# Three bf16 pieces of a matrix for the residuals of a block solve, and other places for TensorE's filler work

## Chip, cores and metric

One core of one Trainium2 chip (trn2). The metric is the device time of one execution in microseconds, as the median of the runs shown.

## What is computed

The reference is two layers of a transformer block on a (4, 256, 256) input. Layer 0 is rotary attention with 16 heads plus a mixture of experts. Layer 1 is a gated delta rule with 16 key heads of two value heads each, plus a feed-forward block with a layer norm. The change lies in layer 1's delta rule:

```python
def step(state, inp):
    q_t, k_t, v_t, b_t, d_t = inp
    state = state * d_t[..., None, None]
    Sk = jnp.einsum('bhi,bhij->bhj', k_t, state)
    delta = (v_t - Sk) * b_t[..., None]
    state = state + jnp.einsum('bhi,bhj->bhij', k_t, delta)
    o = jnp.einsum('bhi,bhij->bhj', q_t, state)
    return (state, o)
```

The kernel does not step through time. For each value head and each chunk of 128 time steps it writes all `delta` at once as the solution W of a unit triangular system, W = V + N W, where N holds the decayed products of keys (the matrix of the system with its sign turned has -1 on its diagonal).

## The kernel before

**Tiling.** Layer 1 runs one `body` for each of the 16 key heads. A head has two value heads (v = 0, 1), four batch entries (b) and two chunks of time (c). `N[v]` is a tile of 128 partitions by 4 x 3 x 128 fp32 columns: for each b the blocks chunk 0 on itself, chunk 1 on chunk 0, chunk 1 on itself. The five engines run their own programs in order and meet at semaphores; the order is written out by hand in one `body` for each engine.

**A head on TensorE** (`body`, L915). The values are turned (L776), the products of keys and queries are made (`products`, L779) while VectorE forms N (`matrices`, L1349) and GpSimd multiplies the decays by the products (`decayed`, L1628). Then `invert` (L793) builds the inverse of the triangular blocks in bf16 in six levels by doubling. In each level TensorE multiplies (L802, L812, L816), VectorE masks (L1380) and ScalarE copies back (L1161, L1165).

**The solve.** The bf16 inverse (`TT`) is only approximate, so each chunk c is solved with two corrections. Stage k = 3c + a, a = 0, 1, 2, goes:
- `apply` (L843): four bf16 matmuls for each v add the inverse times the bf16 right-hand side `Rb[v]` to a PSUM bank, where W builds up over a = 0, 1, 2.
- The bank is copied to `Wv` in fp32: for a = 0 by ScalarE (`first_w`, L1169), for a = 1, 2 by ScalarE for v 0 (`next_w`, L1174) and by VectorE for v 1 (`update`, L1399).
- `residual` (L858), a = 0, 1: four fp32 matmuls for each v of N with `Wv`. An fp32 matmul is two records in the trace.
- `left_over` (L1390) on VectorE: V plus the residual's bank, written in bf16 to `Rb[v]`.
- After a = 2 of chunk 0, `link` (L870, L1441) carries chunk 0 into chunk 1's right-hand side, which ScalarE rounds (`round_r2`, L1179). After chunk 1, `outputs` (L878) multiplies the decayed products with W, and VectorE gates (`gate_o`, L1417).

**Fillers.** So that TensorE has work while the other engines copy, it does parts of the next head between these: projections (`project`, L717; each part two records of 512 columns), the projection of z (`project_z`, L736; halves) and sums of squares (`norms`, L756). The lists `ahead`, `between`, `behind` and `closing` in `body` say which filler stands ahead of the first apply, between the two applies, behind them and behind the residuals of stage k.

**VectorE in the solve.** The convolution of the next head has three taps for each of four channel groups (`conv`, L1327; one instruction L1334 each, with two inputs in SBUF). The third group's taps and the fourth's lie in the last level of the inversion and in the stages k = 0, 1, 2 (`mid` and `end` in VectorE's `body`). `guard` (L1337) turns the sums of squares into reciprocals in stage 3.

**ScalarE in the solve.** It copies out the fourth group's projection (`conv_in(ni, 3)`), squares, and makes the next head's decays (`batch_decays`, L1197). The decays wait for `mask_done` of both v.

**GpSimd** (`body`, L1636), in this order: `decayed` for four b, `scale_y` of the last head's output (L1623), the right-hand side times the norms of the keys (L1647, L1649), the diagonal of N for both v (L1655, `affine_select`, two instructions each), and the masks of the next head's decays (`mask`, L1614; four instructions L1620). In the first head the layer norm's scale, shift and addition follow (`f_tail`, L1663).

## Time and profile before

| what | us |
|---|---|
| median of 3 runs (lowest to highest) | 1804.15 (1802.18 to 1804.24) |
| the profiled execution, its own time | 1804.3 |
| its span in the profile | 1802.3 |
| busy TensorE matmul, VectorE, ScalarE, GpSimd | 1703.3, 1316.0, 1167.9, 652.5 |
| one head of layer 1 (a period of the trace) | 70.4 |

The span runs from the first to the last instruction of the program; the execution's time holds some 2 us beside it. PE is TensorE's matmuls, PEld its weight loads, DVE is VectorE, ACT ScalarE, POOL GpSimd. A matmul's record ends about 0.17 us after its engine can take the next one, so starts tell how long the queue is held.

### The profile page before, as it was taken

The page shows a single profiled execution, that of the slowest core. Times are in us where ns is not written, and L with a number is a line of the kernel's source. Part 1 is how long each engine was busy: PE and PEld are TensorE (multiplying, and loading weights), DVE is VectorE, ACT ScalarE, POOL GpSimd, SP SyncE. Part 2 cuts the span into 40 slices and gives each one's busy share as a digit, 9 for nine tenths or more (in the row PEclk, how much of TensorE's full clock was granted, in tenths as well). Part 3 has the DMA queues.
Part 4 walks back from the last instruction along what each step waited for, and adds up shares of the span by engine and source line. Part 5 has one row for each costly group of instructions (what it writes and reads, how often), then busy time and mean ns, then how long its engine had stood idle before and what let it go on. Part 6 is the DMA issues. An engine that isn't in the chain of part 4 may idle for free.

```text
span 1802.3 us, 34261 instructions
## 1 busy us (share of the span) xinstructions
PE 1703.3 (95%) x13208; PEld 1322.5 (73%) x13208; DVE 1316.0 (73%) x2293; ACT 1167.9 (65%) x2185; POOL 652.5 (36%) x474
## 2 busy tenths in 40 slices
PE   7899999999998987999999999999999999999986
PEld 5676766767665666787787787877877877878875
DVE  7788888888866267767768767777677687677753
ACT  3335353443535465778878878887787788788762
POOL 2222213222214063615516426336246165163340
PEclk9999999999999997999999999999999999999998
DMA  3111010101103200110110101101101201111000
GB/s 138 35 55 47 33 67 33 67 33 55 46 1 105 76 19 1 37 59 25 37 56 28 36 25 60 36 25 37 59 25 36 60 25 36 38 47 36 7 2 24
DMA packets 51447, 75.16 MB, mean 42 GB/s; under 512 B 3392, under 2 KB 41792, under 8 KB 51312
## 3 DMA queue, kind: packets, MB, share of 16 engines
q1 hardware_dynamic: 51312, 73.28, 12.6%
q8 instruction: 94, 1.54, 0.3%
q14 instruction: 41, 0.34, 0.1%
HBM read 72.03 MB, written 1.25 MB: 41 GB/s over the span
## 4 chain that ended last, share of the span: by engine, by line
PE 54%; ACT 7%; DVE 6%; issue 3%; DVEq 0%
PE bank L731 12%; PE bank L911 7%; PE bank L751 5%; PE bank L866 4%; PE bank L789 3%; PE bank L802 2%; PE bank L816 2%; PE bank L812 2%; DVE d_sil L1334 2%; ACT d_dec L1133 2%; PE bank L874 2%; PE bank L887 2%; PE bank L854 2%; PE bank L888 2%; PE bank L889 2%
## 5 line engine op out<-in xcount | busy, mean ns | idle before, releaser
L1634 POOL TENSOR_TENSOR d_dec<-d_dec,d_qk 128x384 f32<-128x384 f32 x128 | 138.8, 1111 | 638.4 <-DVE d_N L1359 571.3
L1334 DVE SCALAR_TENSOR_TENSOR d_sil<-d_pre,d_w,d_sil 128x1024 f32<-128x1024 f32 x192 | 295.2, 1538 | 10.1 <-ACT d_pre L1099 9.9
L731 PE MATMUL bank<-xnT,d_w 128*128 128x512 f32 x480 | 242.4, 617 | 0.0
L189 PE MATMUL bank<-xnT,a_w 128*128 128x512 f32 x512 | 236.6, 596 | 0.0
L1380 DVE CAST_PREDICATED d_X<-tables_sb,bank 128x512 bf16<-128x512 int32 x192 | 134.3, 700 | 89.9 <-PE bank L802 76.4
L1396 DVE TENSOR_TENSOR d_Rb<-d_V,bank 128x512 bf16<-128x512 f32 x128 | 86.5, 685 | 109.8 <-PE bank L866 109.8
L489 POOL TENSOR_TENSOR a_hidc<-a_hid,a_comb 128x512 f32<-128x512 f32 x32 | 44.4, 1387 | 295.0 <-DVE a_hid L336 295.0
L189 PEld LDWEIGHTS bank<-xnT,a_w 128*128 128x128 f32 x512 | 90.6, 192 | 78.5 <-issue 78.5
L1161 ACT ACTIVATE d_T<-bank 128x512 bf16<-128x512 f32 x160 | 100.5, 628 | 65.2 <-PE bank L812 62.6
L866 PE MATMUL bank<-d_W,d_N 128*128 128x128 f32 x1024 | 130.6, 281 | 2.0 <-DVE d_W L1401 1.9
L508 ACT ACTIVATE a_sg<-a_sm 128x384 f32<-128x384 f32 x64 | 33.0, 515 | 152.0 <-DVE a_sm L341 152.0
L751 PE MATMUL bank<-d_w,xnT 128*128 128x256 f32 x512 | 130.1, 388 | 0.0
L911 PE MATMUL bank<-d_wo,d_yT 128*128 128x256 f32 x512 | 127.2, 393 | 0.9 <-ACT d_yT L1194 0.9
L866 PEld LDWEIGHTS bank<-d_W,d_N 128*128 128x128 f32 x1024 | 123.0, 193 | 3.8 <-DVE d_W L1401 2.1
L1165 ACT ACTIVATE d_TT<-bank 128x512 bf16<-128x512 f32 x192 | 119.6, 623 | 2.9 <-PE bank L816 2.9
L481 POOL TENSOR_TENSOR a_qT<-a_rot_a,a_rot_b 128x512 f32<-128x512 f32 x64 | 81.3, 1270 | 100.2 <-DVE a_rot_b L325 100.2
L731 PEld LDWEIGHTS bank<-xnT,d_w 128*128 128x128 f32 x480 | 80.0, 192 | 43.6 <-issue 43.6
L1620 POOL TENSOR_TENSOR d_dec<-d_dec,tables_sb 128x512 f32<-128x512 f32 x64 | 96.8, 1543 | 16.2 <-DMA d_dec<-decay_scratch 16.2
L911 PEld LDWEIGHTS bank<-d_wo,d_yT 128*128 128x128 f32 x512 | 93.7, 193 | 11.8 <-issue 1.2
L1098 ACT ACTIVATE d_sil<-bank,d_w 128x512 f32<-128x512 f32 x128 | 90.1, 704 | 12.8 <-PE bank L983 11.9
L325 DVE SCALAR_TENSOR_TENSOR a_rot_b<-bank,a_w,tables_sb 64x512 f32<-64x512 f32 x128 | 95.9, 750 | 1.9
L751 PEld LDWEIGHTS bank<-d_w,xnT 128*128 128x128 f32 x512 | 90.7, 192 | 8.6
(210 smaller groups left out, 4274.8 us busy)
## 6 DMA issues: line engine op xcount, KB each, us to landing
d_dec<-decay_scratch SPq DMA_DIRECT2D x32, 512.0 KB, 5.7
a_w<-w SPq DMA_DIRECT2D x16, 897.0 KB, 4.6
d_w<-w SPq DMA_DIRECT2D x16, 776.0 KB, 4.6
a_comb<-comb_scratch SPq DMA_DIRECT2D x16, 512.0 KB, 5.6
d_dec<-decay_scratch SPq DMA_DIRECT2D x32, 256.0 KB, 6.1
d_wo<-w SPq DMA_DIRECT2D x16, 256.0 KB, 3.1
f_w<-w SPq DMA_DIRECT2D x8, 256.0 KB, 4.2
x_sb<-x SPq DMA_DIRECT2D x2, 512.0 KB, 4.4
```

Of the source, the lines that this page charges most:

```text
L189: last = pe.matmul(psum[bank][:, :], wq(slot, part, k), xnT[:, k, half * HALF:(half + 1) * HALF], start=(k == 0), stop=(k == KT - 1))
L325: last = dve.scalar_tensor_tensor(two(rot_b[lo:lo + 64, n % 2, :]), two(psum[n][src:src + 64, :]), bias[src:src + 64, :], SN[src:src + 64, ...
L731: last = pe.matmul(psum[bank][:, :], cols(slot, (c * KT + k) * P, P), xnT[:, k, h * HALF:(h + 1) * HALF], start=(k == 0), stop=(k == KT - 1))
L751: last = pe.matmul(psum[n][:, q * 2 * P:(q + 1) * 2 * P], xnT[:, k, t * P:(t + 1) * P], cols(slot, OZ + k * 2 * P, 2 * P), start=(k == 0), ...
L866: last = pe.matmul(psum[5 + 2 * v][:, b * P:(b + 1) * P], N[v][:, b, 2 * c, :], Wv[v][:, b, c, :], start=True, stop=True)
L911: last = pe.matmul(psum[OUT_BANK[n]][:, q * D:(q + 1) * D], yT[v][:, t * P:(t + 1) * P], wo[slot][:, v, :], start=(v == 0), stop=(v == 1))
L1161: act.activation(left(Tm[v][:, :, :], lv).rearrange("p n g w -> p (n g) w"), psum[5 + 2 * v][:, :].rearrange("p (a w) -> p a w", w=lv), AC ...
L1165: act.activation(right(TT[v][:, :, :], lv).rearrange("p n g w -> p (n g) w"), psum[4 + 2 * v][:, :].rearrange("p (a w) -> p a w", w=lv), A ...
L1334: dve.scalar_tensor_tensor(sil[c][:, :, :], pre[c % 2][:, :, tap:tap + S], cols(slot, OC + 4 * c + tap, 1), sil[c][:, :, :], ALU.mult, ALU ...
L1380: dve.copy_predicated(left(Xp[lv][:, v], lv), mask.unsqueeze(1).broadcast_to([P, 8, 64]).rearrange("p n (g w) -> p n g w", w=lv), psum[4 + ...
L1620: last = pool.tensor_tensor(g, g, tabs["future"].unsqueeze(1).broadcast_to([P, B, P]), ALU.add)
L1634: pool.tensor_tensor(g, g, qk[b][:, :, :], ALU.mult).then_inc(s["p_done"], 1)
```

## The change

Three parts.

1. **Residuals in bf16.** The diagonal blocks of N are split into three bf16 pieces: `Nh` (ScalarE casts N, `high`), `Nm` (GpSimd subtracts Nh from N in place and casts the rest, `middle`), `Nl` (GpSimd subtracts Nm from the rest, `lowest`; it takes over the tile `Nb`, so it waits for the last level's corner). Each `apply` now gives a fresh product and not a running sum. The first product is rounded to bf16 (`W0b`), the second is rounded too (`dWb`, `change`), the third stays in PSUM. The first residual is Nh W0b + Nm W0b, the second adds Nl W0b + Nh dWb + Nm dWb in the same bank: 8 and 12 bf16 matmuls of 128 columns for each v in place of 4 fp32 ones. GpSimd adds W0b and dWb (`partial`), and VectorE adds the third product from PSUM (`total`), which `link` and `outputs` wait for.
2. **Fillers.** The list `behind` is replaced by `inner`, between the two residuals. Projections of the fourth group, z halves and norms move by one or two places, so that a stage has one filler between the applies and one between the residuals.
3. **Order on the other engines.** GpSimd's masks are parted: those of v 0 ahead of `middle`, those of v 1 behind `lowest`, ahead of the partial sums. On ScalarE the decays take other places between the copies.

```diff
+        Nh = [m.sb(f"d_Nh{v}", [P, B, 2, P], BF16) for v in range(2)]
+        Nm = [m.sb(f"d_Nm{v}", [P, B, 2, P], BF16) for v in range(2)]
+        Nl = Nb
+        W0b = [m.sb(f"d_W0b{v}", [P, B, P], BF16) for v in range(2)]
+        dWb = [m.sb(f"d_dWb{v}", [P, B, P], BF16) for v in range(2)]
...
                 for b in range(B):
                     last = pe.matmul(psum[4 + 2 * v][:, b * P:(b + 1) * P], TT[v][:, 2 * b + c, :], Rb[v][:, b, :],
-                                     start=(a == 0 and b == 0), stop=(a == 2), skip_group_check=True)
+                                     start=True, stop=True)
...
             def residual(i, v, c, a):
 
                 if a == 0:
                     pe.wait_ge(s["w0_done"], i * 4 + 2 * c + v + 1)
-                    pe.wait_ge(s["diag_done"], i * 2 + v + 1)
+                    pe.wait_ge(s["nm_done"], i * 2 + v + 1)
+                    parts = ((Nh, W0b), (Nm, W0b))
                 else:
-                    pe.wait_ge(s[f"wup_done{v}"], i * 4 + 2 * c + a)
-                for b in range(B):
-                    last = pe.matmul(psum[5 + 2 * v][:, b * P:(b + 1) * P], N[v][:, b, 2 * c, :], Wv[v][:, b, c, :],
-                                     start=True, stop=True)
+                    pe.wait_ge(s["nl_done"], i * 2 + v + 1)
+                    pe.wait_ge(s[f"dw_done{v}"], i * 2 + c + 1)
+                    parts = ((Nl, W0b), (Nh, dWb), (Nm, dWb))
+                for n, (coef, vec) in enumerate(parts):
+                    for b in range(B):
+                        last = pe.matmul(psum[5 + 2 * v][:, b * P:(b + 1) * P], coef[v][:, b, c, :], vec[v][:, b, :],
+                                         start=(a == 0 and n == 0 and b == 0), stop=(a == 1 and n == 2), skip_group_check=True)
...
-                    for c, h, li, half in ((2, 0, 2, 1), (2, 1, 3, 0), (3, 0, 5, 1)):
-                        fill[li][half].append(p(c, h))
+                    for h, (li, half) in enumerate(((2, 1), (3, 0))):
+                        fill[li][half].append(p(2, h))
+                    fill[5][1].append(part(3, 0, 0))
                     z = lambda n, half: (lambda: project_z(nxt[1], nxt[2], n, (half,)))
-                    ahead[0], between[0], behind[0] = [part(3, 1, 0)], [part(3, 1, 1)], [z(0, 0)]
-                    between[1], behind[1] = [z(0, 1)], [q(0, 0)]
-                    between[2], behind[2], closing[2] = [q(0, 1)], [q(1, 0)], [q(1, 1)]
-                    between[3] = [z(1, 0)]
+                    ahead[0], between[0], inner[0] = [part(3, 0, 1)], [part(3, 1, 0)], [part(3, 1, 1)]
+                    between[1], inner[1] = [z(0, 0)], [z(0, 1)]
+                    between[2], inner[2], closing[2] = [z(1, 0)], [q(0, 0)], [q(0, 1)]
+                    between[3], inner[3] = [q(1, 0)], [q(1, 1)]
                     between[4] = [z(1, 1)]
...
                         apply(i, 1, c, a)
-                        for f in behind[k]:
-                            f()
                         for v in range(2):
                             if a < 2:
                                 residual(i, v, c, a)
                             elif c == 0:
                                 link(i, v)
+                            if v == 0:
+                                for f in inner[k]:
+                                    f()
...
+            def high(i, v):
+                act.wait_ge(s["diag_done"], i * 2 + v + 1)
+                act.activation(Nh[v][:, :, :, :], N[v][:, :, 0:3:2, :], ACT.Copy).then_inc(s["nh_done"], 1)
...
+                for v in range(2):
+                    fill[4][v].append(lambda v=v: high(i, v))
...
-                next_w(i, 0, 1)
+                change(i, 0)
                 if nxt:
                     square(ni, 1)
                     batch_decays(ni, ns, 0)
-                    batch_decays(ni, ns, 1)
-                next_w(i, 0, 2)
-                if nxt:
-                    batch_decays(ni, ns, 2)
...
+            def total(i, v, c):
+                dve.wait_ge(s["apply_ready"], i * 12 + 6 * c + 4 + v + 1)
+                dve.wait_ge(s["wsum_done"], i * 4 + 2 * c + v + 1)
+                dve.tensor_tensor(Wv[v][:, :, c, :], Wv[v][:, :, c, :], psum[4 + 2 * v][:, :].rearrange("p (b d) -> p b d", b=B),
+                                  ALU.add).then_inc(s[f"wup_done{v}"], 1)
...
-                        if a:
-                            update(i, c, a)
+                        if a == 1:
+                            change(i, c)
+                        elif a == 2:
+                            for v in range(2):
+                                total(i, v, c)
...
+            def middle(i, v):
+
+                pool.wait_ge(s["nh_done"], i * 2 + v + 1)
+                rest = N[v][:, :, 0:3:2, :]
+                pool.tensor_tensor(rest, rest, Nh[v][:, :, :, :], ALU.subtract).then_inc(s["mid_done"], 1)
+                pool.wait_ge(s["mid_done"], i * 2 + v + 1)
+                pool.tensor_copy(Nm[v][:, :, :, :], rest).then_inc(s["nm_done"], 1)
+
+            def lowest(i, v):
+
+                pool.wait_ge(s["nm_done"], i * 2 + v + 1)
+                pool.wait_ge(s["x_ready"], i * 12 + 2 * len(LEVELS) - 2 + v + 1)
+                pool.tensor_tensor(Nl[v][:, :, :, :], N[v][:, :, 0:3:2, :], Nm[v][:, :, :, :],
+                                   ALU.subtract).then_inc(s["nl_done"], 1)
+
+            def partial(i, v, c):
+
+                pool.wait_ge(s["w0_done"], i * 4 + 2 * c + v + 1)
+                pool.wait_ge(s[f"dw_done{v}"], i * 2 + c + 1)
+                pool.tensor_tensor(Wv[v][:, :, c, :], W0b[v][:, :, :], dWb[v][:, :, :], ALU.add).then_inc(s["wsum_done"], 1)
...
                 if nxt:
-                    mask(*nxt)
+                    mask(*nxt, 0)
+                for v in range(2):
+                    middle(i, v)
+                for v in range(2):
+                    lowest(i, v)
+                if nxt:
+                    mask(*nxt, 1)
+                for c in range(2):
+                    for v in range(2):
+                        partial(i, v, c)
                 if isinstance(i, int) and i == 0:
                     f_tail()
```

## Rows read from the trace of the kernel before

**Rows 1.** The page's first line.
```profile
span 1802.3 us, 34261 instructions
```

**Rows 2.** Windows: busy us of each engine over one head, granted clock, DMA share, GB/s.
```profile
1049.20:1119.64 70.44, 68.56 (x663) 55.84 (x659) 51.90 (x77) 57.54 (x103) 31.14 (x22) 1.00 0.12 39
```

**Rows 3.** Timeline of TensorE in one head's solve: start, length, records.
```profile
1125.07 1.95 PE L866 MATMUL bank<-d_W,d_N 128*128 128x128 f32 x16
...
1126.90 0.40 PE L854 MATMUL bank<-d_Rb,d_TT 128*128 128x128 bf16 x4
...
1134.17 2.05 PE L874 MATMUL bank<-d_W,d_N 128*128 128x128 f32 x16 [0.38 <-ACT d_W L1176]
...
1136.90 0.39 PE L854 MATMUL bank<-d_Rb,d_TT 128*128 128x128 bf16 x4
...
1140.16 0.40 PE L854 MATMUL bank<-d_Rb,d_TT 128*128 128x128 bf16 x4
1140.39 1.08 PE L751 MATMUL bank<-d_w,xnT 128*128 128x256 f32 x4
1141.31 0.39 PE L854 MATMUL bank<-d_Rb,d_TT 128*128 128x128 bf16 x4
...
1144.66 0.44 PE L887 MATMUL bank<-d_W,d_dec 128*128 128x128 f32 x2
```

**Rows 4.** Timeline of ScalarE in level 4 of the inversion, idle time in brackets.
```profile
1117.51 0.60 ACT L1161 ACTIVATE d_T<-bank 128x512 bf16<-128x512 f32 x1 [1.66 <-PE bank L812]
```

**Rows 5.** Timelines of GpSimd and VectorE in the same head, single instructions and groups.
```profile
1098.64 1.04 POOL L1647 TENSOR_TENSOR d_Rb<-d_V,d_knorm 128x512 bf16<-128x512 f32 x1
...
1111.04 0.63 POOL L1655 TENSOR_SCALAR_AFFINE_SELECT d_N<-d_N 128x512 f32<-128x512 f32 x1
...
1111.64 2.23 POOL L1620 TENSOR_TENSOR d_dec<-d_dec,tables_sb 128x512 f32<-128x512 f32 x1
...
1111.64 5.93 POOL L1620 TENSOR_TENSOR d_dec<-d_dec,tables_sb 128x512 f32<-128x512 f32 x4
...
1111.11 1.63 DVE L1334 SCALAR_TENSOR_TENSOR d_sil<-d_pre,d_w,d_sil 128x1024 f32<-128x1024 f32 x1
...
1118.59 1.28 DVE L1334 SCALAR_TENSOR_TENSOR d_sil<-d_pre,d_w,d_sil 128x1024 f32<-128x1024 f32 x1
```

**Rows 6.** One line's instructions over the whole trace: ns min/median/max, first and last start.
```profile
L1620 POOL TENSOR_TENSOR d_dec<-d_dec,tables_sb x64: 1260/1272/2251, 576.1 to 1679.8; 128x512 f32<-128x512 f32 x64
...
L1682 POOL COPY d_X<-d_identb x12: 1036/1040/1041, 548.1 to 558.9; 128x1024 bf16<-128x1024 bf16 x12
...
L1626 POOL TENSOR_TENSOR x_sb<-x_sb,d_yrs x32: 1886/1896/1899, 742.7 to 1782.9; 128x1024 f32<-128x1024 f32 x32
...
L1396 DVE TENSOR_TENSOR d_Rb<-d_V,bank x128: 673/686/690, 689.6 to 1770.6; 128x512 bf16<-128x512 f32 x128
...
L1151 ACT ACTIVATE d_Nb<-d_N x32: 1048/1051/1059, 655.0 to 1728.2; 128x1024 bf16<-128x1024 f32 x32
```

**Rows 7.** Timelines of GpSimd and VectorE in the first head.
```profile
695.05 4.51 POOL L1667 TENSOR_TENSOR x_sb<-x_sb,f_gamma 128x2048 f32<-128x2048 f32 x1 [19.36 <-DVE x_sb L1460]
...
705.11 5.39 POOL L1671 TENSOR_TENSOR acc_sb<-acc_sb,x_sb 128x2048 f32<-128x2048 f32 x1
...
695.49 5.15 DVE L1334 SCALAR_TENSOR_TENSOR d_sil<-d_pre,d_w,d_sil 128x1024 f32<-128x1024 f32 x1
...
723.64 0.69 DVE L1423 TENSOR_TENSOR x_sb<-d_gated,bank 128x512 f32<-128x512 f32 x1 [0.70 <-PE bank L889]
```

**Rows 8.** Windows of the first and last head; the third-last number is the granted clock.
```profile
663.20:678.20 15.00, 8.87 (x160) 6.26 (x160) 14.90 (x28) 10.49 (x21) 12.49 (x8) 1.00 0.00 1
678.30:685.00 6.70, 5.36 (x36) 3.04 (x37) 3.32 (x6) 4.85 (x6) 0.00 (x0) 0.50 0.01 2
1754.00:1773.00 19.00, 15.20 (x141) 13.42 (x139) 9.75 (x15) 6.41 (x11) 0.00 (x0) 1.00 0.00 1
```

More of the change, by code:

```diff
@@ L907, in project_out @@
                     pe.wait_ge(s["pre_done"], nxt[2] * 8 + 4 + n - 1)
-                for q in range(2):
+                for q in parts:
                     t = 2 * n + q
@@ L933, in body @@
                         fill[li][half].append(lambda n=n: project_out(*before, n, nxt))
-                ahead, between, behind, closing = ([[] for _ in range(6)] for _ in range(4))
+                ahead, between, inner, closing = ([[] for _ in range(6)] for _ in range(4))
                 if nxt:
@@ L1494, in body @@
                     mid[2] = [cv(3, 2)]
-                    end[3] = [lambda: guard(ns, ni)]
+                    end[3].append(lambda: guard(ns, ni))
                 if first:
@@ L1613, in _, with mask @@
         def _(pool):
-            def mask(j, slot, i):
+            def mask(j, slot, i, v):
                 pool.wait_ge(dec_in[slot], j * 64 + 64)
-                for v in range(2):
-                    for c in (0, 2):
-                        g = dec[slot][v][:, :, c, :]
-                        last = pool.tensor_tensor(g, g, tabs["future"].unsqueeze(1).broadcast_to([P, B, P]), ALU.add)
-                    last.then_inc(s["mask_done"], 1)
+                for c in (0, 2):
+                    g = dec[slot][v][:, :, c, :]
+                    last = pool.tensor_tensor(g, g, tabs["future"].unsqueeze(1).broadcast_to([P, B, P]), ALU.add)
+                last.then_inc(s["mask_done"], 1)
             def scale_y(i, v):
@@ L1634, in decayed, with diagonal @@
                     pool.tensor_tensor(g, g, qk[b][:, :, :], ALU.mult).then_inc(s["p_done"], 1)
+            def diagonal(i, v):
+                pool.wait_ge(s["nb_done"], i * 2 + v + 1)
+                pool.wait_ge(s["tt1_done"], i * 2 + v + 1)
+                for c in (0, 2):
+                    n = N[v][:, :, c, :]
+                    last = pool.affine_select(n, n, pattern=[[0, B], [-1, P]], base=0, channel_multiplier=1,
+                                              compare_op=ALU.not_equal, fill=-1.0)
+                last.then_inc(s["diag_done"], 1)
+            def middle(i, v):
[13 more added lines that the diff above has]
+                pool.tensor_tensor(Wv[v][:, :, c, :], W0b[v][:, :, :], dWb[v][:, :, :], ALU.add).then_inc(s["wsum_done"], 1)
             def body(j, slot, i):
@@ L1682, in _ @@
                     pool.tensor_copy(Xp[lv][:, v, :, :], identb[:, :].unsqueeze(1).broadcast_to([P, 8, P])).then_inc(ev["ident_done"], 1)
-            mask(0, 0, 0)
+            for v in range(2):
+                mask(0, 0, 0, v)
             loop(pool, body)
```

43 lines of the change are left out of this document (19 added, 24 removed).

## The prediction, made before the changed kernel was run

> **What bounds the kernel now.** First the page: one core, a span of 1802.3 us [rows 1]. Then a window over one head of layer 1: 70.44 us, of which TensorE is busy 68.56, VectorE 51.90, ScalarE 57.54 and GpSimd 31.14 [rows 2]. So TensorE bounds a head, and GpSimd looks idle for more than half of it. That share is an average. The timeline of GpSimd shows that its work lies in one piece and that its last masks begin at 1111.64 and run for 5.93 us [rows 5]; behind them it sleeps until the next head. The solve is later: the first pair of residuals starts at 1125.07, the link of the two halves at 1134.17, the first apply of the second half at 1136.90 and the outputs at 1144.66 [rows 3]. I use this head's clock from here on.
>
> **What TensorE saves.** A pair of fp32 residuals (sixteen records) holds the queue from 1125.07 to 1126.90, 1.83 us [rows 3]. Four bf16 matmuls of the same 128 columns hold it for 0.23 (the apply from 1140.16, the filler behind it at 1140.39) [rows 3], 0.056 each. The new pairs have 16 and 24 of these: 0.90 and 1.34 us. A head has two pairs of each kind: 7.32 before, 4.48 after, 2.8 us less work. It is a gain only where nothing else is late. The fillers keep their number and are moved by a place or two; one lasts 0.92 (1140.39 to 1141.31) [rows 3].
>
> **Small terms.** ScalarE gets two castings of 1024 columns a head, 1.05 each [rows 6], behind the diagonal, in level 4 of the inversion. There it idles, 1.66 us before the copy at 1117.51 alone [rows 4]: nothing, as long as these gaps stand; without them each would delay the inversion by 1.05. It loses two copies. VectorE loses two copies and gains four totals of the kind that the residual subtraction has, 0.69 each [rows 6]. The last two lie on the path between the last apply and the outputs.
>
> **What GpSimd gains, and its price.** Behind the diagonal now stand, in this order: two masks, casting work for both v (subtract, copy, subtract, copy), two subtractions for the lowest piece, the other two masks, and four partial sums, of which two belong to the first half of the solve. A subtraction of 1024 columns with two full inputs is not in the trace. The mask adds 512 columns in 1.27 [rows 6]; right behind a release it needs 1.13 (below), so 0.14 is spent ahead of the data and 1024 columns cost 2.4. Bounds: 1.04, what a copy of 1024 bf16 columns takes, and 2.4; with one broadcast input 1024 columns took 1.90 [rows 6]. I take 2.4, since both inputs are full tiles. The copy to bf16 costs 1.04 by the nearest row, 1.90 at most. A partial sum costs 1.27, between 1.04 (the scaled 512 columns written in bf16 [rows 5]) and 1.5.
>
> **The term that decides: the taps of the convolution.** Look at 1111.04. GpSimd's diagonal takes 0.63, to 1111.67. The tap that VectorE starts at 1111.11 ends only at 1112.74, 1.07 after it; in the clear, at 1118.59, it takes 1.28 [rows 5]. The mask that GpSimd starts at 1111.64 ends at 1113.87, 1.13 after the tap [rows 5]. So the two never overlap: one holds the other off for its whole length, and with both waiting they alternate. The same shows in the first head: beside a GpSimd instruction of 4.51 a tap takes 5.15 [rows 7]. In the kernel before, a head's last six taps, from 1118.59 on, run while GpSimd sleeps. After the change the first five of them run against it. Each adds 1.07 + 0.04 - 0.14, some 1.0, to GpSimd's row, and waits itself for up to 2.4.
>
> **GpSimd's row, added up.** The first two masks end at 1113.87 and, 1.23 later, at 1115.1. Behind them: four subtractions 9.6, two copies 2.1, two masks 2.5, two partial sums 2.5, together 16.8, less 0.04 of overlap ten times, plus five taps (the third channel group's three and the fourth's first two) at 1.0: 21.3 us. The second partial sum of the first half ends at **1136.4**, the first at 1134.2. Without taps it would be 1131.5. The middle pieces are ready at 1118.5 and 1122.9, ahead of the residuals at 1125; the lowest ones at 1125.2 and 1128.6, ahead of theirs at 1129 and 1131; the last masks at 1133, which holds back ScalarE's decays (2.9 with their table load, an estimate from ScalarE's place in the queue) but not yet the rounding of the second half. So what is late is the totals. The fourth group's second tap ends at 1135.3, the first total at 1136.0, and the link of v 0 starts there instead of at 1134.17. Then come a filler, the link of v 1 (its total is ready at 1137.1) and a filler: 2 x 0.92 of links and 2 x 0.92 of fillers, and the first apply of the second half starts at 1139.7 instead of 1136.90: **+2.8 us a head**. The 1.4 us saved by two residual pairs and the filler that is already behind are in this number: TensorE has waited them away.
>
> **The second half.** From that apply to the next stage: two applies 0.45, two fillers 1.84, two short residuals 0.90, so 3.2 against 3.26. The next stage has one filler: apply and filler to 1.15, the change of v 1 is in PSUM 0.42 after its start and copied 0.69 later, at 2.3; its residual (0.67 and 0.2 until it is read) ends at 3.2, the subtraction at 3.9, the total of v 0 starts 0.1 before that and ends at 4.5. Before, 4.50. No change: the latency of the total eats the residual's gain.
>
> **First and last head.** In the first, the layer norm's three instructions on GpSimd (from 695.05 to 710.50 [rows 7]) now stand behind the partial sums, so behind the second half. The taps that they held up for some 10 us run free, TensorE is at the outputs some 10 us sooner, near 712; but the gating needs their end: 15.4 us behind 711.5 is 727, against 723.64 [rows 7], and then its four instructions run without gaps. Net +1, between -3 and +5. The last head has no taps, masks or fillers: shorter residuals against waits for partial sums, 0, between -2 and +1.
>
> **Sum.** 14 heads at +2.8 are +39, first head +1: 1804.3 (the profiled execution, 2.0 above its span; the median of runs is 1804.15) gives 1844.
>
> **A page's price.** The Trainium skill (GPSIMD Engine Reference, section 3.1) gives some 2.6 cycles at 1.2 GHz per element for two inputs, a floor that comes from its one read port, and names no type. By it the subtraction would take 2.2 us (an estimate from that page), 0.2 under the value taken, and the sum would be 1838; it speaks against the first rival below. No row here has a bf16 input in such an instruction.
>
> **Rivals.** (1) *GpSimd reads bf16 cheaper*: at 1.90 the four subtractions are 2.0 sooner, and the taps fall elsewhere: +0.8 to +2.1 a head, 1816 to 1834, about 1826. For it: the broadcast row. Against: full tiles stand at 2.4. (2) *GpSimd is in time* (the other side): place, the totals of the first half, which VectorE could reach at 1132.0 and 1132.6 if no tap waited. It decides if the second partial sum ends by 1132.6, that is if a subtraction costs 1.1 or less. Then the saved residuals count in the first half alone, -0.45 a head, and -1 in the last: 1797. At 1.3 it is no change. For it: a copy of the same size takes 1.04. Against: every instruction with two inputs. (3) *The clock falls as well*: TensorE would idle 1.0 before the second residual pair and 2.1 before the link. In the first head the granted clock was 0.50 (1.2 GHz) for 6.70 us after 15 us in which TensorE was busy for 8.87; in the last head it stayed 1.00 through 19 us with 15.20 busy [rows 8]. If it fell once a head, 6.7 us at half speed cost some 3.4 more: 1892. (4) *Slower castings*: at 1.9 for the copy, 1.7 more directly and up to 2 a head in all: up to 1868. (5) That the change doesn't do what it says: in PSUM the pieces accumulate over the v's bank in an open group; if they ran at fp32's pace (0.11 a record) the pairs would cost 1.8 and 2.7, and the sum hardly moves since TensorE waits there anyway.
>
> **Chances.** Forecast, with (4), 0.55; (1) 0.17; (3) 0.08; (2) faster 0.12; within the bound 0.08. About 0.2% (3.6 us) is what a measurement of this kernel tells from none. The forecast's own range is 1830 to 1868; the range given reaches down to 1801 for (1) and for no change, and up to 1876 for a slow copy with waits of its own. What it leaves out is (2) and (3), 0.20 together.
>
> **What would show it.** Right: in the head's window GpSimd busy about 52 us (31.14, 16.8 of new work, four to five blocked); taps of 2 to 3.5 us; VectorE's totals of the first half waiting for GpSimd's partial sum; TensorE idle ahead of the link; a head of 73.2. Wrong: subtractions near 1.1, or the link released by VectorE alone with no wait for GpSimd; residual pairs longer than 0.9 and 1.34; idle of TensorE ahead of the first residual pair (then the middle piece is late); a granted clock under 1.00 within the heads.

## The result and the profile after

| | median, us | lowest to highest | ratio to before, 95% interval |
|---|---|---|---|
| before | 1803.16 (4 runs) | 1800.60 to 1804.24 | |
| changed | 1828.31 (4 runs) | 1826.44 to 1829.46 | 1.0141 [1.0123, 1.0158] |

The change makes the kernel 25 us slower, where 40 were forecast. The profiled execution took 1829.21 us, 24.9 above that of before.

The page of the changed kernel, in the parts that answer to [rows 1] and to the taps and masks of [rows 5, 6]:

```profile
span 1827.1 us, 35189 instructions
...
PE 1667.5 (91%) x13464; PEld 1275.6 (70%) x13464; DVE 1387.6 (76%) x2325; ACT 1183.1 (65%) x2185; POOL 959.4 (53%) x634
...
L1348 DVE SCALAR_TENSOR_TENSOR d_sil<-d_pre,d_w,d_sil 128x1024 f32<-128x1024 f32 x192 | 349.0, 1818 | 10.1 <-ACT d_pre L1111 9.8
...
L1687 POOL TENSOR_TENSOR d_W<-d_W0b,d_dWb 128x512 f32<-128x512 bf16 x64 | 88.4, 1391 | 136.2 <-ACT d_dWb L1192 131.8
```

TensorE has 36 us less to do than before and still ends 25 us later. GpSimd has 307 us more (959.4 against 652.5). The 192 taps, which the change doesn't touch, took 295.2 us before and take 349.0.

**Where the 25 us lie.** I cut the span at each head's turn of the values. Windows from turn to turn (the columns of [rows 2]; layer 0, the first head, two later heads, the last head):

```profile
0.00:640.09 640.09, 608.46 (x2793) 427.01 (x2794) 488.71 (x1071) 267.37 (x591) 149.70 (x123) 0.99 0.17 56
640.09:724.69 84.60, 63.52 (x626) 48.96 (x624) 54.64 (x92) 56.73 (x98) 57.26 (x33) 0.90 0.03 11
...
870.43:944.07 73.64, 67.77 (x674) 54.42 (x673) 57.25 (x78) 58.48 (x102) 50.94 (x32) 0.98 0.12 37
...
1089.76:1161.82 72.06, 66.21 (x674) 52.84 (x673) 57.29 (x78) 58.48 (x102) 50.95 (x32) 1.00 0.12 38
...
1741.82:1827.09 85.27, 60.80 (x642) 52.12 (x640) 41.67 (x69) 38.71 (x67) 39.26 (x30) 0.90 0.04 13
```

Before, all 14 heads between the first and the last took 70.43 to 70.45. Now a head takes 72.06, and five of the 14 take 73.63 to 73.67 at a granted clock of 0.98 (one more takes 72.42). In four of the five the clock falls at the link; the first of them only takes over a fall that began in TensorE's wait at the end of the first head. The 14 together: 1017.1 against 986.1, +31.0. Of these 14 x 1.62 = 22.7 are in every head, and the other 8.3 in those six: 7.9 in the five with the lower clock, 0.4 in the one of 72.42, whose clock is 1.00. The rest is -1.5 in layer 0 (whose code is the same), -1.3 in the first head and -3.5 in the last: 31.0 - 6.2 = 24.8, the difference of the spans.

**Inside a head.** GpSimd's timeline behind the diagonal (start, length, what it does, count):

```profile
1121.77 3.48 POOL L1642 TENSOR_TENSOR d_dec<-d_dec,tables_sb 128x512 f32<-128x512 f32 x2
1125.19 2.14 POOL L1672 TENSOR_TENSOR d_N<-d_N,d_Nh 128x1024 f32<-128x1024 f32 x1
1127.40 1.04 POOL L1674 CAST d_Nm<-d_N 128x1024 bf16<-128x1024 f32 x1
1128.40 2.13 POOL L1672 TENSOR_TENSOR d_N<-d_N,d_Nh 128x1024 f32<-128x1024 f32 x1
1130.59 1.91 POOL L1674 CAST d_Nm<-d_N 128x1024 bf16<-128x1024 f32 x1
1132.47 5.21 POOL L1680 TENSOR_TENSOR d_Nb<-d_N,d_Nm 128x1024 bf16<-128x1024 f32 x2
1137.63 4.46 POOL L1642 TENSOR_TENSOR d_dec<-d_dec,tables_sb 128x512 f32<-128x512 f32 x2
1142.06 3.24 POOL L1687 TENSOR_TENSOR d_W<-d_W0b,d_dWb 128x512 f32<-128x512 bf16 x2
```

There is no gap from 1121.77 to 1145.30, where before the engine slept behind its last mask [rows 5]. VectorE in the same stretch:

```profile
1128.72 2.88 DVE L1348 SCALAR_TENSOR_TENSOR d_sil<-d_pre,d_w,d_sil 128x1024 f32<-128x1024 f32 x1
...
1132.72 2.95 DVE L1348 SCALAR_TENSOR_TENSOR d_sil<-d_pre,d_w,d_sil 128x1024 f32<-128x1024 f32 x1
...
1142.38 1.92 DVE L1348 SCALAR_TENSOR_TENSOR d_sil<-d_pre,d_w,d_sil 128x1024 f32<-128x1024 f32 x1
1144.22 0.68 DVE L1420 TENSOR_TENSOR d_W<-d_W,bank 128x512 f32<-128x512 f32 x1
1145.41 0.69 DVE L1420 TENSOR_TENSOR d_W<-d_W,bank 128x512 f32<-128x512 f32 x1 [0.52 <-POOL d_W L1687]
```

A tap that takes 1.28 in the clear waits out a GpSimd instruction. The first total is behind such a tap, the second waits for the partial sum itself. TensorE, in answer to [rows 3]:

```profile
1134.81 0.39 PE L875 MATMUL bank<-d_W0b,d_Nh 128*128 128x128 bf16 x4
1135.03 0.39 PE L875 MATMUL bank<-d_W0b,d_Nm 128*128 128x128 bf16 x4
1135.25 1.08 PE L736 MATMUL bank<-xnT,d_w 128*128 128x512 f32 x2
...
1139.31 0.38 PE L875 MATMUL bank<-d_W0b,d_Nb 128*128 128x128 bf16 x4 [1.17 <-ACT d_dWb L1192]
...
1144.95 1.16 PE L883 MATMUL bank<-d_W,d_N 128*128 128x128 f32 x8 [1.79 <-DVE d_W L1420]
...
1148.61 0.40 PE L859 MATMUL bank<-d_Rb,d_TT 128*128 128x128 bf16 x4
...
1156.36 0.49 PE L896 MATMUL bank<-d_W,d_dec 128*128 128x128 f32 x2 [0.20 <-DVE d_W L1420]
```

Counted from the first mask (1111.64 before, 1121.77 after): the link starts at 23.18 (before 22.53), the second half at 26.84 (25.26), the outputs at 34.59 (33.02). So 0.65 is lost ahead of the link and 0.93 at the filler that now stands between the links; the second half costs what it did. TensorE's idle time ahead of the link, in the table of waits (sum, how often, longest):

```profile
PE bank L883 <- DVE d_W L1420: 25.2, 15, 1.8
```

**A second wait, in the last level of the inversion.** The kernel before has nothing like it at this place. TensorE waits 1.21 us for VectorE's last mask, in every head:

```profile
1132.26 0.41 PE L821 MATMUL bank<-d_TT,d_X 128*128 128x64 bf16 x8 [1.21 <-DVE d_X L1394]
```

The same in the table of waits:

```profile
PE bank L821 <- DVE d_X L1394: 18.0, 15, 1.2
```

The mask runs on VectorE from 1131.53, right behind the tap that starts at 1128.72 and takes 2.88 in place of 1.28: GpSimd's second subtraction holds the tap off. The idle times above 0.15 us of such a head sum to 5.8, before to 1.8; the rest of the head, TensorE's work, is 2.36 shorter. That is the 1.62. GpSimd's row has no gap and the totals wait for it, so a TensorE without this wait would only idle longer at the link (argued from the rows). It tells once the row is shorter (e7 and e11 below).

**The slower heads.** Windows around the link of such a head; the third-last number is the granted clock:

```profile
923.00:925.90 2.90, 1.11 (x9) 0.78 (x8) 2.56 (x3) 1.29 (x4) 2.90 (x2) 1.00 0.02 6
925.90:929.30 3.40, 3.40 (x18) 3.40 (x18) 2.48 (x3) 0.63 (x1) 0.08 (x1) 0.50 0.00 0
```

TensorE idles for 1.79 us ahead of the link (and for 1.17 some 6 us earlier), and then its clock is 0.50 of full speed (1.2 GHz) for 3.40 us. Half of that, 1.7, would be lost; the head is 1.58 longer.

### The profile page after: what moved, and what is told of

Read it like the earlier page. It is cut to its first block, busy times and chain, and to the rows that moved or that the text cites. A ratio compares the mean times of both kernels' runs of the same rounds, so it can differ in the third digit from the quotient of the medians.

```text
span 1827.1 us, 35189 instructions
## 1 busy us (share of the span) xinstructions
PE 1667.5 (91%) x13464; PEld 1275.6 (70%) x13464; DVE 1387.6 (76%) x2325; ACT 1183.1 (65%) x2185; POOL 959.4 (53%) x634
## 3 DMA queue, kind: packets, MB, share of 16 engines
HBM read 72.03 MB, written 1.25 MB: 40 GB/s over the span
## 4 chain that ended last, share of the span: by engine, by line
PE 49%; DVE 9%; issue 5%; ACT 4%; POOL 3%; DVEq 0%; POOLq 0%
PE bank L736 10%; PE bank L920 5%; PE bank L756 4%; DVE d_sil L1348 3%; PE bank L766 3%; PE bank L794 3%; DVE d_X L1394 2%; POOL d_W L1687 2%; PE bank L807 2%; PE bank L875 2%; PE bank L883 2%; PE bank L817 2%; PE bank L821 2%; PE bank L896 2%; PE bank L781 2%
## 5 line engine op out<-in xcount | busy, mean ns | idle before, releaser
L1348 DVE SCALAR_TENSOR_TENSOR d_sil<-d_pre,d_w,d_sil 128x1024 f32<-128x1024 f32 x192 | 349.0, 1818 | 10.1 <-ACT d_pre L1111 9.8
L1687 POOL TENSOR_TENSOR d_W<-d_W0b,d_dWb 128x512 f32<-128x512 bf16 x64 | 88.4, 1391 | 136.2 <-ACT d_dWb L1192 131.8
L1642 POOL TENSOR_TENSOR d_dec<-d_dec,tables_sb 128x512 f32<-128x512 f32 x64 | 124.0, 1958 | 16.3 <-DMA d_dec<-decay_scratch 16.3
L1145 ACT ACTIVATE d_dec<-d_dec,d_gcol 128x256 f32<-128x256 f32 (+1 forms) x256 | 93.2, 443 | 10.0 <-POOL d_dec L1642 9.9
```

Source lines behind the costliest of these rows:

```text
L1348: dve.scalar_tensor_tensor(sil[c][:, :, :], pre[c % 2][:, :, tap:tap + S], cols(slot, OC + 4 * c + tap, 1), sil[c][:, :, :], ALU.mult, ALU ...
L1642: last = pool.tensor_tensor(g, g, tabs["future"].unsqueeze(1).broadcast_to([P, B, P]), ALU.add)
L1687: pool.tensor_tensor(Wv[v][:, :, c, :], W0b[v][:, :, :], dWb[v][:, :, :], ALU.add).then_inc(s["wsum_done"], 1)
```

## The experiments

"Head" is the window from turn to turn of a head without a fall of the clock (for e2 the shortest kind; four of its heads without a fall take 72.2). Before 70.44, changed 72.06.

| kernel | median, us | ratio to before [95%] | head |
|---|---|---|---|
| e1 filler places alone | 1821.72 | 1.0108 [1.0091, 1.0125] | 71.70 |
| e2 changed, old filler places | 1842.38 | 1.0232 [1.0207, 1.0256] | 71.79 |
| e3 one more subtraction | 1888.27 | 1.0477 [1.0460, 1.0495] | 75.8 (all with a fall) |
| e4 changed, narrow taps | 1780.50 | 0.9878 [0.9862, 0.9895] | 69.30 |
| e5 before, narrow taps | 1797.19 | 0.9971 [0.9960, 0.9983] | 70.44 |
| e6 before, with idle GpSimd work | 1810.71 | 1.0050 [1.0033, 1.0066] | 71.04 |
| e7 two pieces | 1816.04 | 1.0074 [1.0057, 1.0091] | 71.12 |
| e8 running sum, no partial sums | 1815.10 | 1.0070 [1.0053, 1.0087] | 71.30 |
| e9 two pieces directly, running sum | 1777.01 | 0.9857 [0.9841, 0.9873] | 68.82 |
| e10 as e9, old filler places | 1784.35 | 0.9896 [0.9880, 0.9911] | 69.05 |
| e11 two pieces directly, partial sums | 1794.34 | 0.9953 [0.9939, 0.9968] | 70.03 |
| e12 TensorE kept busy | 1829.69 | 1.0145 [1.0129, 1.0161] | 72.05 |

**The two halves of the change, each alone (e1, e2).** e1 is the kernel before with the new lists; e2 the changed kernel with the old ones:

```diff
-                    for c, h, li, half in ((2, 0, 2, 1), (2, 1, 3, 0), (3, 0, 5, 1)):
-                        fill[li][half].append(p(c, h))
+                    for h, (li, half) in enumerate(((2, 1), (3, 0))):
+                        fill[li][half].append(p(2, h))
+                    fill[5][1].append(part(3, 0, 0))
...
-                        for f in behind[k]:
-                            f()
...
+                            if v == 0:
+                                for f in inner[k]:
+                                    f()
```

> The kernel before with the change's filler places alone, fp32 residuals kept. Theory A (GpSimd's row of work and its mutual exclusion with the taps make the loss): the fillers alone are no part of it. But working the stages through with rows of before, the second residual pair now waits for ScalarE's copy, which stands behind the later projection copy, and a fp32 residual follows: I get 1.4 us a head, +20 us, so about 1824. Theory B (the new order of the fillers is what costs, and the splitting pays nothing back): +25 or more, the whole loss. If the order is neutral: 1804 within 3.

> The changed kernel with the filler places of before. Theory A: GpSimd's last partial sum ends where it did, so little moves: 0.3 us a head sooner, 1823 against 1828. Theory B: the loss goes, 1800 to 1806.

e1 landed near its number, with a reason of its own. TensorE's timeline of its solve:

```profile
1141.72 1.16 PE L874 MATMUL bank<-d_W,d_N 128*128 128x128 f32 x8 [1.33 <-ACT d_W L1178]
...
1145.34 0.39 PE L854 MATMUL bank<-d_Rb,d_TT 128*128 128x128 bf16 x4
...
1153.90 0.44 PE L887 MATMUL bank<-d_W,d_dec 128*128 128x128 f32 x2
```

From the link to the outputs it needs 12.18 us against 10.49 [rows 3]: two more fillers stand between them (five, before three). What they leave in the first half isn't gained: TensorE idles 1.33 ahead of the link, since ScalarE reaches its copy only behind 2.88 us of decays. With fp32 residuals the new places alone cost 1.26 a head.

e2 missed: 1842, not 1823. Without a fall of the clock its head, 71.79, is even 0.27 shorter than the changed kernel's. But where the clock falls, it falls for twice as long. Windows of one quiet head and one such head, and the stretch of the fall:

```profile
1093.25:1165.04 71.79, 67.16 (x675) 53.02 (x673) 57.35 (x78) 58.35 (x102) 51.00 (x32) 1.00 0.13 38
...
1309.00:1383.10 74.10, 69.94 (x674) 56.12 (x673) 58.45 (x78) 58.49 (x102) 49.91 (x32) 0.95 0.12 37
```

```profile
1363.10:1369.90 6.80, 6.80 (x36) 6.80 (x36) 5.28 (x6) 0.63 (x1) 0.46 (x1) 0.50 0.00 0
```

Five heads took 74.1 to 76.7, in the fastest of the four executions (1836.61; the others reach 1846.70). So in this kernel the old places cost more by the clock than they save. What in e2 makes the falls longer was not settled; with less work on GpSimd the old places cost far less (e10).

**One GpSimd instruction more (e3).**

```diff
                 for v in range(2):
                     lowest(i, v)
+                pool.tensor_tensor(Tm[0][:, :, :].rearrange("p (b c) d -> p b c d", b=B), N[0][:, :, 0:3:2, :],
+                                   Nm[0][:, :, :, :], ALU.subtract)
```

> The changed kernel with one more GpSimd subtraction of 1024 columns per head behind the lowest pieces, whose result nobody reads. Theory A: it stands in the row that the totals wait for, 2.1 us a head in 15 heads, +30, 1858 (more if the clock falls more often). Theory B, or any in which GpSimd has room: 1828 within 4.

Also a miss, by 30 us: slower than expected, as e2 was. TensorE at the link, and the head:

```profile
1010.52 0.40 PE L859 MATMUL bank<-d_Rb,d_TT 128*128 128x128 bf16 x4 [0.75 <-DVE d_Rb L1410]
...
1015.15 1.98 PE L883 MATMUL bank<-d_W,d_N 128*128 128x128 f32 x8 [3.09 <-DVE d_W L1420]
```

```profile
957.79:1033.60 75.81, 67.87 (x674) 54.40 (x673) 58.20 (x78) 58.44 (x102) 53.02 (x33) 0.98 0.13 36
```

The idle time is 3.84 in place of 1.79: 2.05, the price of one subtraction, arrives at TensorE whole. So a longer row on GpSimd moves the link by what it is longer. What I had not put into the expectation is the clock: it now falls in every head, 1.6 us each or more (75.8 - 72.06 = 2.05 + 1.7).

**Taps with next to no data (e4 in the changed kernel, e5 in the one before).**

```diff
-                    dve.scalar_tensor_tensor(sil[c][:, :, :], pre[c % 2][:, :, tap:tap + S], cols(slot, OC + 4 * c + tap, 1),
-                                             sil[c][:, :, :], ALU.mult, ALU.add).then_inc(s["conv_step"], 1)
+                    n_cols = 8 if c > 1 else S
+                    dve.scalar_tensor_tensor(sil[c][:, :, 0:n_cols], pre[c % 2][:, :, tap:tap + n_cols],
+                                             cols(slot, OC + 4 * c + tap, 1),
+                                             sil[c][:, :, 0:n_cols], ALU.mult, ALU.add).then_inc(s["conv_step"], 1)
```

> The changed kernel with the convolution's taps of the two value channel groups cut to 8 of 256 columns per batch entry: that much of the convolution is left out. Theory A: nothing blocks GpSimd from the last level on, the row ends some 5 us sooner, the totals wait for nobody, and TensorE keeps what the bf16 residuals save: 3.2 us a head less than the changed kernel, no falls of the clock, about 1775. Theory B: only VectorE's own time is saved, which the same cut in the kernel before must then show too.

> The control for the narrow taps: the same cut (the value groups' taps at 8 of 256 columns, the rest of that convolution left out) in the kernel before. Theory A: TensorE and ScalarE set a head's length there and the taps are hidden, so 1803 within 5. Theory B: as much is saved here as in the changed kernel, some 40 us.

The same cut is worth 47.8 us to the changed kernel and 5.5 to the one before (1802.69 beside it), whose heads stay at 70.44 and gain only in the first one (82.28 against 85.88). In e4 the head is 69.30, and of the 14 only the first, behind the wait at the end of the first head, is longer (71.54). So the loss is not GpSimd's new work alone but that work and the taps together. Both waits go: the one ahead of the link from 1.79 to 0.17, the one in the last level from 1.21 to 0.19. VectorE and GpSimd in e4 also show what kind of meeting it is:

```profile
1106.74 1.86 DVE L1349 SCALAR_TENSOR_TENSOR d_sil<-d_pre,d_w,d_sil 128x32 f32<-128x32 f32 x1
...
1119.37 0.24 DVE L1349 SCALAR_TENSOR_TENSOR d_sil<-d_pre,d_w,d_sil 128x32 f32<-128x32 f32 x1
```

```profile
1106.42 2.14 POOL L1674 TENSOR_TENSOR d_N<-d_N,d_Nh 128x1024 f32<-128x1024 f32 x1
```

Thirty-two columns take 0.24 us alone. Started at 1106.74, behind a subtraction that ends at 1108.56, they end at 1108.60. The tap isn't slowed by its own size; it is held off until the other engine is done.

**GpSimd's load without its results (e6).** The kernel before, with ten unread instructions of the new kinds behind the masks:

```diff
                     mask(*nxt)
+                    for n in range(10):
+                        need(pool, s["spare_done"], i * 10 + n - 1)
+                        if n < 4:
+                            last = pool.tensor_tensor(Xc[n % 2][:, :, :, :], Xa[:, :, :, :], Xb[:, :, :, :], ALU.subtract)
+                        elif n < 6:
+                            last = pool.tensor_copy(Xc[n % 2][:, :, :, :], Xa[:, :, :, :])
+                        else:
+                            last = pool.tensor_tensor(Xc[n % 2][:, :, 0, :], Xa[:, :, 0, :], Xb[:, :, 0, :], ALU.add)
+                        last.then_inc(s["spare_done"], 1)
```

> The kernel before with the change's GpSimd work as a dummy behind the masks: four subtractions of 1024 columns, two copies, four additions of 512, on tiles of their own, results read by nobody. It parts blocking from waiting. Theory A: the taps are blocked as in the changed kernel but no total waits; by the rows that delays the second stage's taps and the copies behind them by 0.8 us a head, +11, about 1815. If the whole loss came from blocked taps: 1828. If blocking costs nothing: 1803.

```profile
1080.93:1151.95 71.02, 68.72 (x658) 55.87 (x657) 54.39 (x76) 57.50 (x102) 51.87 (x32) 1.00 0.12 38
```

GpSimd is as busy as in the changed kernel (51.87), and the head loses only 0.6. So taps that wait on GpSimd, with nobody waiting for GpSimd, cost little in this placement. It is not quite that of the changed kernel: the load begins 5.9 us behind the first mask and not 3.4, the last level's tap takes 2.16 and not 2.88, and TensorE has a filler more ahead of the last mask, so the wait in the last level is absent. e6 doesn't price that part.

**Less on GpSimd's row (e7, e8, e11, e9).** e7 leaves out the lowest piece. e8 lets W build up in PSUM again, takes dWb as PSUM minus W0b, and drops the partial sums:

```diff
-                    parts = ((Nl, W0b), (Nh, dWb), (Nm, dWb))
+                    parts = ((Nh, dWb), (Nm, dWb))
...
-                for v in range(2):
-                    lowest(i, v)
```

> The changed kernel with two bf16 pieces in place of three: no lowest piece, its two subtractions and its eight matmuls in a stage with a = 1 left out. Theory A: GpSimd's row is 4.3 us shorter, but the blocked taps stay: 0.8 us a head and the falls of the clock, 1811 to 1817. Theory C (the many bf16 matmuls are what costs): 0.9 us a head for the matmuls alone, in every head, whatever GpSimd does.

```diff
-                                     start=True, stop=True)
+                                     start=(a == 0 and b == 0), stop=(a == 2), skip_group_check=True)
...
+                dve.tensor_tensor(dWb[v][:, :, :], psum[4 + 2 * v][:, :].rearrange("p (b d) -> p b d", b=B), W0b[v][:, :, :],
+                                  ALU.subtract).then_inc(s[f"dw_done{v}"], 1)
...
-                for c in range(2):
-                    for v in range(2):
-                        partial(i, v, c)
```

> The changed kernel with W built up in PSUM over the three applies as before: the change dWb is PSUM less W0b on VectorE for both v, the last copies are plain ones, one on ScalarE and one on VectorE, and GpSimd's partial sums are gone. Theory A: the totals no longer wait for GpSimd, but the last masks and the lowest pieces still run against the taps, and VectorE has one more instruction ahead of the second residuals: 0.5 us a head less than the changed kernel, 1815 to 1821. If the partial sums are the whole story: 1790.

Each of the two takes off 12 to 13 us, no more. e7 by itself can't tell theory A from theory C: its head is 0.94 shorter, and the 16 matmuls that it leaves out in a head hold the queue for 16 x 0.056 = 0.9. Against theory C stand e3, e4 and e8, which have the changed kernel's matmuls and move its head by +3.7, -2.8 and -0.8. And e7 shows something else. GpSimd's partial sums, VectorE's tap and TensorE's link in e7:

```profile
1132.28 3.32 POOL L1686 TENSOR_TENSOR d_W<-d_W0b,d_dWb 128x512 f32<-128x512 bf16 x2 [3.37 <-ACT d_dWb L1191]
...
1134.83 1.86 DVE L1347 SCALAR_TENSOR_TENSOR d_sil<-d_pre,d_w,d_sil 128x1024 f32<-128x1024 f32 x1
...
1137.33 1.16 PE L882 MATMUL bank<-d_W,d_N 128*128 128x128 f32 x8 [1.68 <-DVE d_W L1419]
```

GpSimd is early here and sleeps 3.37 us ahead of the partial sums, yet TensorE idles 1.68 ahead of the link, almost as long as before. The totals stand behind a tap that the second partial sum holds off, and the whole chain is late by the 1.21 of the last level, which e7 still has. So in the changed kernel a second limit lies close behind GpSimd's row: a longer row costs its whole length (e3), 4.3 us less of it bring the link only 0.6 nearer to the head's start (54.59 against 55.19). In e8 the wait ahead of the link is gone with the partial sums and the totals, and the one in the last level stays (1.22).

e11 is e7 with the middle piece written in bf16 by the subtraction itself (this edit), and e9 is e11 and e8 together:

```diff
-                pool.tensor_tensor(rest, rest, Nh[v][:, :, :, :], ALU.subtract).then_inc(s["mid_done"], 1)
-                pool.wait_ge(s["mid_done"], i * 2 + v + 1)
-                pool.tensor_copy(Nm[v][:, :, :, :], rest).then_inc(s["nm_done"], 1)
+                pool.tensor_tensor(Nm[v][:, :, :, :], rest, Nh[v][:, :, :, :], ALU.subtract).then_inc(s["nm_done"], 1)
```

> Two pieces written straight, with the change's partial sums and totals kept. Theory A: the partial sums end early enough, but two totals per chunk on VectorE and the tap between them stay on the path: 0.2 us a head less than the kernel before, 1796 to 1802. If GpSimd's row is all that counts: as the kernel without partial sums, 1777 to 1786.

> The changed kernel with two pieces, the second written as bf16 straight by GpSimd's subtraction (no copy), W built up in PSUM and no partial sums: GpSimd's new work is two subtractions of 1024 columns a head. Theory A: its row ends 11 us earlier, it blocks two taps for a little, nothing waits for it, and TensorE keeps the shorter residuals: 1.3 us a head less than the kernel before, 69.1, and 5 us in the first and last head: 1777 to 1786, faster than both. Theory C (the bf16 residuals do not pay by themselves): 1800 or more.

GpSimd in e9, and its head:

```profile
1102.32 3.47 POOL L1642 TENSOR_TENSOR d_dec<-d_dec,tables_sb 128x512 f32<-128x512 f32 x2
1105.75 4.22 POOL L1672 TENSOR_TENSOR d_Nm<-d_N,d_Nh 128x1024 bf16<-128x1024 f32 x2
1109.94 3.48 POOL L1642 TENSOR_TENSOR d_dec<-d_dec,tables_sb 128x512 f32<-128x512 f32 x2
```

```profile
1070.31:1139.13 68.82, 65.49 (x659) 51.85 (x657) 54.26 (x78) 58.22 (x103) 36.33 (x24) 1.00 0.13 40
```

The row ends at 1113.42, 11.1 us behind the first mask and not 23.5. The link (at 1122.58) has no idle time ahead of it, and no head of the 14 has a fall. This version beats the kernel before by 1.4% and the changed one by 2.8%. It keeps two pieces of N where the change keeps three, so of the 3.24 that its head is shorter than the changed kernel's, 0.9 is TensorE's own work (16 x 0.056, an estimate). e11 came out 2 us under its range. From e9 to e11 the partial sums and totals add 1.21 a head. From e11 to e7 the two copies add 1.09: their only trace on TensorE is the wait in the last level, which e11 doesn't have and e7 has. From e7 to the changed kernel the lowest piece adds 0.94, about what its matmuls take.

**The filler places again (e10).** As e9, with the lists of before (the edit of e2).

> The same with the filler places of the kernel before. With GpSimd out of the way, the places should matter little: 0.2 us a head more than with the new ones, 1780 to 1789. If the new places are what makes the bf16 residuals pay: 1795 or more.

With GpSimd out of the way the new places gain 7 us: 0.23 in every head (69.05 to 68.82, 3.3 us in 14) and as much again because e10 has two heads with a fall (70.69 and 70.70) and e9 none.

**TensorE kept busy (e12).**

```diff
                         apply(i, 1, c, a)
+                        if k == 2:
+                            for n in range(24):
+                                pe.matmul(psum[5][:, 0:P], identb[:, :], Rb[0][:, 0, :], start=True, stop=True)
```

> The changed kernel with 24 bf16 matmuls of 128 columns that nobody reads, in the idle time of TensorE ahead of the link (1.34 of the 1.79 us). They add work and no wait. If the falls of the clock in four link stages come from this idle time, they go: 6 us less, about 1822. If the falls come from elsewhere: 1828, or more if the work is in the way.

```profile
1141.99 1.50 PE L979 MATMUL bank<-d_Rb,d_identb 128*128 128x128 bf16 x24
1143.94 1.16 PE L883 MATMUL bank<-d_W,d_N 128*128 128x128 f32 x8 [0.44 <-DVE d_W L1423]
```

```profile
725.90:800.59 74.69, 70.17 (x697) 56.56 (x697) 58.21 (x80) 59.82 (x103) 50.94 (x32) 0.96 0.12 36
800.59:872.64 72.05, 67.53 (x699) 54.17 (x698) 57.26 (x78) 58.49 (x102) 50.93 (x32) 1.00 0.12 38
...
1737.55:1827.34 89.79, 65.88 (x666) 56.56 (x664) 41.66 (x69) 38.73 (x67) 39.22 (x30) 0.88 0.04 13
```

Two things were to be told apart, and the total alone would have misled. The mechanism is as expected: of the 14 heads, 12 take 72.03 to 72.06, and only the first of them (which follows the wait at the end of the first head) and one of 72.39 are longer; the 14 sum to 1011.7, against 1017.1 in the changed kernel. So the falls come from the idle time ahead of the link. The expected 6 us did not show in the median, since in this execution the first head takes 1.3 more and the last one 4.5 more than in the changed kernel's. Half of the last head's 4.5 is its final projection, 9.39 us against 7.14 at a lower granted clock (0.76 against 1.00). The last head varies among kernels that have the same work in it: 88.73 (before), 89.27 (e1), 87.50 (e5), 86.98 (e6). What sets the clock there in a given kernel was not settled.

## Why the prediction was right, and where it was off

**Direction and mechanism: right for the link.** The forecast was +2.8 in each of 14 heads, from totals that wait for GpSimd's row. They do: TensorE idles 1.79 ahead of the link (2.1 predicted), the second total waits 0.52 for its partial sum, GpSimd is busy for 50.95 a head (about 52 predicted). e3 shows that a subtraction more in the row costs its full length, and e4 and e5 that the taps decide with it: with narrow taps the new residuals, all three pieces, gain 1.1 a head (69.30 against 70.44).

**What it had not seen.** The prediction let the taps be held off, but of what stands behind a tap on VectorE it looked at the totals only. The last level's mask stands behind one too, and TensorE waits 1.21 for it. Among its signs of being wrong was idle time ahead of the first residual pair, put down to a late middle piece; the idle time is there, with this other cause. It did not change the number, as the link waited longer still, but it is why e7 gains so little. And TensorE's work fell by 2.35 a head in the windows (68.55 to 66.20), not by 2.8; where the rest stays was not traced.

**Size: the step that was off is the price of the subtraction.** It was scaled from the mask [rows 6] to 2.40 and is 2.13; a partial sum was taken as 1.27 and is 1.15. Four subtractions and two sums: 4 x 0.27 + 2 x 0.12 = 1.3. The row was to end 24.8 behind the first mask and ends at 23.5, those 1.3 sooner. The link was to start at 24.4 and starts at 23.2. That takes the head from +2.8 to +1.6. The price that the prediction took from the Trainium skill (GPSIMD Engine Reference, section 3.1) as an estimate, 2.2 with a sum of 1838, was nearer on both counts. Its sum does not follow, though: by the prediction's own row, 0.2 less for each of four subtractions is 0.8 a head and gives 1833. Nor is the section without a type: it measures an fp32 addition of 2048 columns at 4.50 us. The layer norm's fp32 instruction of 2048 columns here takes 4.51 [rows 7], so the trace agrees; half of that, 2.26, was a row nearer to the truth than the mask and was passed over. I had kept to the nearest row although it has other types; 2.13 lies between the copy (1.04) and that row, in the upper part, as the range had it.

**The parts that held.** The copy: 1.04. The residual pairs: 0.44 and 0.67 for each v by the starts (1134.81 to 1135.25, and 1139.31 to the filler at 1139.98), so 0.9 and 1.34 a pair as worked out. The second half: 7.75 from first apply to outputs, before 7.76, no change. The ScalarE castings cost nothing. The idle time ahead of the second residual pair: 1.17, predicted 1.0. In the first head the outputs start at 711.12 (near 712 predicted).

**Luck in the number.** The forecast's own range was 1830 to 1868. The measured 1828 lies just under it, in the part that was added for rival (1) and for no change. And it is a sum of errors on both sides: 7.9 us of clock that the forecast left out, against -1.5 in layer 0 and -4.8 in the first and last head. The heads alone, without the falls, give +22.7 where 39 were forecast.

**First and last head.** The gating of the first head starts at 723.85, not at 727: the three instructions of the layer norm run back to back in 13.7 us, from 710.03 to 723.72. I had kept their 15.4, which contained waits for taps (0.9 in the last of them alone [rows 7]) that I had just moved away. The last head was to be 0 and is -3.5. From its turn to the end of the outputs it is 1.8 shorter, but that can't be put down to the shorter residuals: in e4, whose last head has the same instructions, the way from the turn to the final projection takes 74.03, in the kernel before 74.12, in the changed one 72.29. The other 1.6 is the final projection, 7.14 us against 8.77 at a granted clock of 1.00 against 0.81; e5 and e6, which lack the change, have 7.14 too. So neither part is shown to be the change's. Together -4.8 against +1.

**Rivals.** (1), a cheaper subtraction, had 1.90 and 1826 us; at 2.13 the truth is between it and the forecast, and the median (1828) nearer to its number. But its number is partly reached by another way: without the falls of the clock the heads would give 8 us less. (2) is out: the row would have to end 21.0 behind the first mask and ends at 23.5. e7 adds that this condition is not enough: its partial sums end 20.9 behind the first mask, and its head is still 0.7 longer than before. (3), the clock, was said to cost 3.4 in each head; it costs 1.6 in four of 14 at the link, and as much in a fifth by a fall that began in the first head. A granted clock under 1.00 within the heads was named as a sign of being wrong, and 7.9 of the 25 us are that. I had read the last head's window, where 19 us with 15.20 busy kept 1.00 [rows 8], as a sign against it. e12 shows its cause. (4) and (5) are out by the rows above; at the 2 a head that (4) names, its bound would have been 1872 and not 1868.

**Sum.** Forecast +40: 39 in the heads and 1 in the first. Measured +24.8 in the spans: 22.7 in every head, 7.9 by the clock, 0.4 in one head at full clock, -1.3 first head, -3.5 last, -1.5 in layer 0.

## What to carry to other kernels

Work that is moved to an engine with idle time has to be placed on that engine's timeline from the moment its inputs are there: 20.7 us of it cost 0.6 a head where nobody waited for its end (e6 against before), 2.1 us cost 2.05 and the clock where the link did (e3 against the changed kernel). Price such a row instruction by instruction, with what excludes it on other engines. Then look at everything that stands behind a held-off instruction, not only at the last reader: here a mask in the inversion waited too, and shortening the row alone (e7) gained little until that wait (e11) and the partial sums (e9) went as well. And if a wait on TensorE grows, look for the clock behind it: in e3 2.1 us of waiting cost 3.7.

## What the runs showed of the hardware

- **A VectorE tap and a GpSimd instruction exclude each other, whatever the tap's size.** The taps have two inputs in SBUF. One with 32 columns, 0.24 us in the clear, took 1.86 behind a GpSimd subtraction (e4). Adds and subtractions with two SBUF inputs, and by the 1.91 for a cast that takes 1.04 alone, one-input casts too, wait for a tap in the same way. The Trainium skill says so (SBUF — State Buffer, Who interferes with whom): a VectorE instruction with two inputs in SBUF and a GpSimd instruction that reads SBUF take turns for their whole length. The traces agree.
- **GpSimd's prices**, 128 partitions: subtraction of 1024 columns, fp32 minus bf16, 2.13 us whether it writes fp32 or bf16; sum of 512 bf16 with bf16 columns 1.15 to 1.16; of 512 fp32 with fp32 1.27 [rows 6]; cast of 1024 columns 1.04. A subtraction that writes bf16 at once saves the cast.
- **Short waits can halve TensorE's clock.** After idle times of 1.17 and 1.79 us in one stretch of the solve, the granted clock was 0.50 for 3.40 us in four heads and stayed 1.00 in others with the same waits; with 3.09 in place of 1.79 it fell in every head (e3); with 24 unread matmuls in the wait it stayed 1.00 in 13 of 14 heads (e12), the other one following the wait at the end of the first head.
